# Attention scores in three banks, maxima moved by transfer alone, rows turned 13 images later

## The reference

```python
qkv = (xt @ W_fc.T + b_fc).reshape(bs, n, HEADS, 3 * D)
q, k, v = jnp.split(qkv, 3, axis=-1)
attn = jnp.einsum('bihd,bjhd->bijh', q, k) * scale
attn = jax.nn.softmax(attn, axis=2)
out = jnp.einsum('bijh,bjhd->bihd', attn, v).reshape(bs, n, HEADS * D)
out = out @ W_last.T + b_last + xt
```

## Time and profile before

| | us |
|---|---|
| three runs | 867.73, 867.62, 866.97 (median 867.62) |
| the profiled execution | 864.95 |
| its span, first to last instruction | 863.2 |
| PE busy, of the span | 688.5 (80%) |
| DVE busy | 612.1 (71%) |
| ACT busy | 418.2 (48%) |
| POOL busy | 424.5 (49%) |
| scores by query, first and last product start (L586) | 79.8 and 395.6 |

### The profile page before, as it was taken

One profiled execution on the slowest core, in us unless ns is written; L12 is line 12 of the kernel. 1 busy time (PEld: TensorE's weight loads), 2 busy tenths in 40 slices (PEclk: granted clock), 3 DMA queues, 4 the chain that ended last, 5 costly groups with the idle time before them and its releaser, 6 DMA issues. The chain is left out here.

```text
span 863.2 us, 21250 instructions
## 1 busy us (share of the span) xinstructions
PE 688.5 (80%) x7173; PEld 521.9 (60%) x7173; DVE 612.1 (71%) x1648; ACT 418.2 (48%) x829; POOL 424.5 (49%) x560
## 2 busy tenths in 40 slices
PE   0658899999999999997746998784988787359994
PEld 0234566666666666665545887762666666349993
DVE  3765578788877777876598888767567776647764
ACT  0355466665655544553264666520766666134442
POOL 0236102222227888879405777702555787724551
PEclk9979999999999999999566999985999999669995
DMA  6740000000000000000001222413400000122216
GB/s 175 225 164 1 2 3 2 3 3 3 2 3 4 3 15 15 21 16 21 25 1 34 53 53 54 47 7 106 119 2 2 14 17 17 53 68 72 65 46 195
DMA packets 42316, 37.39 MB, mean 43 GB/s; under 512 B 8947, under 2 KB 34536, under 8 KB 42212
## 3 DMA queue, kind: packets, MB, share of 16 engines
q1 hardware_dynamic: 35300, 24.55, 10.0%
q0 software_dynamic: 4800, 9.40, 4.8%
q10 hardware_dynamic: 2112, 2.10, 0.8%
HBM read 26.76 MB, written 9.46 MB: 42 GB/s over the span
## 5 line engine op out<-in xcount | busy, mean ns | idle before, releaser
L782 DVE TENSOR_REDUCE attend_negmax<-ps 128x4 f32<-128x1024 f32 (+1 forms) x128 | 139.6, 1090 | 82.9 <-PE ps L586 82.2
L729 ACT ACTIVATE attend_prob<-ps 128x1024 f32<-128x1024 f32 (+1 forms) x128 | 110.7, 865 | 137.2 <-PE ps L596 137.2
L586 PE MATMUL ps<-attend_key,attend_query 32*128 32x256 f32 (+2 forms) x1024 | 124.8, 360 | 12.8 <-DVE attend_negmax L782 11.6
L596 PE MATMUL ps<-attend_query,attend_key 32*128 32x256 f32 (+2 forms) x1024 | 124.6, 359 | 1.1 <-ACT attend_prob L729 1.0
L586 PEld LDWEIGHTS ps<-attend_key,attend_query 32*128 32x128 f32 x1024 | 79.6, 184 | 53.5 <-issue 45.7
L1777 POOL DMA_INDIRECT sums_xs<-table,sums_source x79 | 76.6, 969 | 56.8 <-DVE sums_source L1710 33.0
L596 PEld LDWEIGHTS ps<-attend_query,attend_key 32*128 32x128 f32 x1024 | 88.3, 184 | 2.3 <-issue 2.2
L1495 PE MATMUL ps<-sums_xT,sums_own 128*128 128x128 f32 x632 | 84.0, 279 | 0.0
L1495 PEld LDWEIGHTS ps<-sums_xT,sums_own 128*128 128x128 f32 x632 | 78.3, 195 | 0.0
L522 POOL TENSOR_SCALAR attend_rstd<-attend_spread 128x2 f32<-128x2 f32 x32 | 7.5, 234 | 130.7 <-DVE attend_spread L837 130.7
L1838 ACT ACTIVATE sums_hidden<-ps 128x512 f32<-128x512 f32 x79 | 47.2, 597 | 34.2 <-PE ps L1495 34.1
(11 more groups left out here) (346 smaller groups left out, 1616.7 us busy)
## 6 DMA issues: line engine op xcount, KB each, us to landing
attend_query<-attend_negmaxT SPq DMA_DIRECT2D x512, 0.5 KB
w<-in_L_ffn_w SPq DMA_DIRECT2D x1, 4096.0 KB, 27.9
expert_xs<-slots SPq DMA_DIRECT2D x39, 64.5 KB, 1.9
x<-in_x ACTq DMA_DIRECT2D x4, 512.0 KB, 8.3
table<-rows SPq DMA_DIRECT2D x16, 128.0 KB
experts<-in_L_ffn_W SPq DMA_DIRECT2D x1, 2048.0 KB, 8.7
experts<-in_L_ffn_W SPq DMA_DIRECT2D x4, 512.0 KB, 9.6
rows<-outputs SPq DMA_DIRECT2D x8, 256.0 KB, 4.9
```

The costliest lines, as they stand in the source:

```text
L586: return nc.tensor.matmul(ps[:, SCORE + i, at:at + width], query[rows, n % 3, odd, a * 128:(a + 1) * 128], key[rows, n % 3, odd, from_:fro ...
L596: return nc.tensor.matmul(ps[:, KEY_SCORE + i, at:at + width], key[rows, n % 3, odd, b * 128:(b + 1) * 128], query[rows, n % 3, odd, from_ ...
L729: nc.scalar.activation(of_pair(t // 4, t % 4)[:, :, 0:wide], ps[:, KEY_SCORE:KEY_SCORE + 2, 0:wide], ACT.Exp).then_inc(prob_ready, 1)
L782: last = nc.vector.tensor_reduce(out=negmax[:, s % 2, 0:4].rearrange("p (a r) -> p r a", a=2), in_=ps[:, SCORE:SCORE + 2, 0:2 * width].rea ...
```

## The change

Both kinds of scores get three banks in turn where banks are free: scores by query use banks 0 to 2 throughout; scores by key use 3, 4 and 7 in the first 48 slots, and 3 and 4 after that. TensorE then waits for one head of the slot before instead of for both, VectorE reduces each head by itself, and ScalarE takes the exponentials head by head in the first 48 slots. Bank 7 is TURN: the dense layer's rows are turned 13 images later instead of 5, and the gate's logits use it too. VectorE no longer transposes the maxima: SyncE sends them straight from 128 partitions into the query's row, in the dense layer two transfers a slot of 128 pieces of two numbers (query columns are then read in steps of two), in the windowed layer four of 128 pieces of one number. ScalarE copies the values out at j = 0, and their bias is multiplied by the output weights once, in the preparation, and added to the output's bias. The gate's products move from j = 2 to j = 0 and their copy from j = 3 to j = 1.

```diff
-    SCORE, KEY_SCORE, PROJECT, HEADS, TURN, MISC = 0, 2, 4, 5, 6, 7
+    SCORE, KEY_SCORE, PROJECT, HEADS, TURN = 0, 3, 5, 6, 7
+    KEY_BANKS = (KEY_SCORE, KEY_SCORE + 1, TURN)
+    BY_HEAD = 4 * (IMAGES - 4)
+    BEHIND = 13
...
+        def key_bank(t, i):
+
+            return KEY_BANKS[(2 * t + i) % 3] if t < BY_HEAD else KEY_SCORE + i
+
+        def exponentials(t):
+
+            return 2 * min(t, BY_HEAD) + max(t - BY_HEAD, 0)
+
+        def score_bank(s, i):
+
+            return SCORE + (2 * s + i) % 3
+
...
+        def placed(k):
+
+            return 32 * min(k, IMAGES) + 64 * max(k - IMAGES, 0)
...
-                    sp.wait_ge(max_turned, s + 1)
                     for i in range(2):
                         row = free_row(groups[i], odd)
+                        sp.wait_ge(max_ready, 2 * s + i + 1)
+                        if not windowed(n):
+                            sp.dma_start(query[row:row + 1, n % 3, odd, :], negmax[:, s % 4, i, :])\
+                                .then_inc(max_placed[s % 4], 16)
+                            continue
                         for a in range(2):
                             sp.dma_start(query[row:row + 1, n % 3, odd, a * 128:(a + 1) * 128],
-                                         negmaxT[2 * a + i::32, s % 4, :]).then_inc(max_placed[s % 4], 16)
+                                         negmax[:, s % 4, i, a:a + 1]).then_inc(max_placed[s % 4], 16)
...
                         if s >= 1 and not windowed(n):
-                            pe.wait_ge(max_ready, s)
+                            pe.wait_ge(max_ready, 2 * s - 1)
...
-                        return nc.tensor.matmul(ps[:, SCORE + i, at:at + width],
-                                                query[rows, n % 3, odd, a * 128:(a + 1) * 128],
+                        own = slice(a * 128, (a + 1) * 128) if windowed(n) else slice(a, N, 2)
+                        return nc.tensor.matmul(ps[:, score_bank(s, i), at:at + width],
+                                                query[rows, n % 3, odd, own],
...
-                            pe.wait_ge(prob_ready, t)
+                            pe.wait_ge(prob_ready, 2 * t - 1 if t < BY_HEAD else exponentials(t))
...
                     if s >= 1:
-                        pe.wait_ge(max_ready, s)
+                        pe.wait_ge(max_ready, 2 * s - 1)
...
+                def free_turn(n):
+
+                    if n == IMAGES - 3:
+                        pe.wait_ge(prob_ready, exponentials(BY_HEAD))
+                    if n - 6 >= IMAGES:
+                        pe.wait_ge(rowsT_ready, min(n - 5 - IMAGES, IMAGES))
+                        pe.wait_ge(logits_taken, min(n - 5 - IMAGES, IMAGES))
+
+                def turn_in(k):
+                    pe.wait_ge(rows_ready, k + 1)
+                    if k >= 1:
+                        pe.wait_ge(in_ready, k)
+                    for a in range(2):
+                        mm = nc.tensor.transpose(ps[:, TURN, a * 128:(a + 1) * 128], rows[:, 2 * k + a, 0:C], ident)
+                    mm.then_inc(in_turned, 1)
...
+                        if runs(n - 6) and windowed(n - 6):
+                            gate_logits(n - 6)
...
-                        if runs(n - 6) and windowed(n - 6):
-                            gate_logits(n - 6)
-                        if runs(n - 5):
+                        if n >= BEHIND:
+                            free_turn(n)
+                        if 0 <= n - BEHIND < IMAGES:
+                            turn_in(n - BEHIND)
+                        if runs(n - 5) and windowed(n - 5):
                             turn_rows(n - 5)
...
+                def take_values(n):
+                    act.wait_ge(v_projected, n + 1)
...
+                    for a in range(2):
+                        last = nc.scalar.activation(
+                            vaug[:, n % 3, a, :, :, 0:16],
+                            ps[:, PROJECT, a * 128:(a + 1) * 128].rearrange("p (r g d) -> p g r d", g=2, d=D), ACT.Copy)
+                    last.then_inc(vaug_ready, 1)
+
                 def exponential(t):
...
+                    if t < BY_HEAD:
+                        for i in range(2):
+                            act.wait_ge(key_scored[i], t + 1)
+                            nc.scalar.activation(to[:, i], ps[:, key_bank(t, i), 0:wide], ACT.Exp)\
+                                .then_inc(prob_ready, 1)
+                    else:
+                        for i in range(2):
+                            act.wait_ge(key_scored[i], t + 1)
+                        nc.scalar.activation(to, ps[:, KEY_SCORE:KEY_SCORE + 2, 0:wide], ACT.Exp).then_inc(prob_ready, 1)
...
+                    if j == 0 and runs(n):
+                        take_values(n)
                     if j == 3:
-                        if runs(n - 5):
+                        if 0 <= n - BEHIND < IMAGES:
+                            take_in(n - BEHIND)
+                        if runs(n - 5) and windowed(n - 5):
                             take_rows(n - 5)
...
-                    last = nc.vector.tensor_reduce(out=negmax[:, s % 2, 0:4].rearrange("p (a r) -> p r a", a=2),
-                                                   in_=ps[:, SCORE:SCORE + 2, 0:2 * width].rearrange(
-                                                       "p r (a n) -> p r a n", a=2),
-                                                   axis=AX.X, op=ALU.max, negate=True)
-                    last.then_inc(max_ready, 1)
-
-                def turn_max(s):
-                    dve.wait_ge(max_ready, s + 1)
-                    if s >= 4:
-                        dve.wait_ge(max_placed[s % 4], 64 * (s // 4))
-                    nc.vector.transpose(negmaxT[:, s % 4, :], negmax[:, s % 2, :]).then_inc(max_turned, 1)
+                    for i in range(2):
+                        dve.wait_ge(scored[i], s + 1)
+                        nc.vector.tensor_reduce(out=negmax[:, s % 4, i, :],
+                                                in_=ps[:, score_bank(s, i), 0:2 * width].rearrange(
+                                                    "p (a n) -> p a n", a=2),
+                                                axis=AX.X, op=ALU.max, negate=True).then_inc(max_ready, 1)
...
                 def add_out(n):
                     dve.wait_ge(out_projected, n + 1)
+                    dve.wait_ge(vaug_ready, min(n + 5, COUNT))
...
+                    pe.wait_ge(biased, 2)
+                    nc.tensor.matmul(ps[:, 5, 0:C], v_bias[:], wo[0][:], start=True, stop=True).then_inc(turned, 1)
...
                     dve.wait_ge(turned, 2)
+                    nc.vector.tensor_copy(v_bias[:], ps[:, 4, 2:3].to_broadcast([128, 128])).then_inc(biased, 1)
...
-                    nc.vector.tensor_copy(v_bias[:], ps[:, 5, 0:128])
+                    dve.wait_ge(turned, 3)
+                    nc.vector.tensor_tensor(o_bias[:, 0, :], o_bias[:, 0, :], ps[:, 5, 0:C], ALU.add)
```

More of the change, by code:

```diff
@@ L362, in _, with attend @@
                             widen(b)
-def attend(nc, xf, tokens, rows, table, weights, consts, query_scales, key_scales, v_bias, o_bias, window_mask, gate,
+def attend(nc, xf, tokens, rows, table, weights, consts, query_scales, key_scales, o_bias, window_mask, gate,
            logits, choice, ps):
@@ L415, in attend @@
         vaug_ready = sem("vaug_ready")
-        scored = sem("scored")
+        scored = [sem(f"scored{i}") for i in range(2)]
         max_ready = sem("max_ready")
-        max_turned = sem("max_turned")
         max_placed = [sem(f"max_placed{r}") for r in range(4)]
-        key_scored = sem("key_scored")
+        key_scored = [sem(f"key_scored{i}") for i in range(2)]
         prob_ready = sem("prob_ready")
@@ L758, in _ @@
             def _(dve):
-                def take_values(n):
-                    dve.wait_ge(v_projected, n + 1)
-                    if n >= 4:
-                        dve.wait_ge(out_projected, n - 3)
-                    if n == 0:
-                        dve.wait_ge(zeros_set, 3)
-                    if n >= 3:
-                        dve.wait_ge(weighted, 2 * n - 4)
-                    for a in range(2):
-                        out = vaug[:, n % 3, a, :, :, 0:16]
-                        got = ps[:, PROJECT, a * 128:(a + 1) * 128].rearrange("p (r g d) -> p g r d", g=2, d=D)
-                        if windowed(n):
-                            last = nc.vector.tensor_copy(out, got)
-                        else:
-                            last = nc.vector.tensor_tensor(
-                                out, got, v_bias[:].rearrange("p (r g d) -> p g r d", g=2, d=D), ALU.add)
-                    last.then_inc(vaug_ready, 1)
@@ L867, in _ @@
                     if j == 1:
-                        if runs(n):
-                            take_values(n)
                         if runs(n - 3):
                             invert_sums(n - 3)
+                        if runs(n - 6) and windowed(n - 6):
```

(21 more changed lines are left out.)

73 lines of the change are left out of this document (38 added, 35 removed).

## The result

The changed kernel takes 875.6 us (874.92 to 877.11, four runs) against 867.3 before: 1.0106 times as long, 95% interval 1.0079 to 1.0133. The forecast was 848.2, the range 835 to 868. It is slower, by the mechanism of the rival that named SyncE.

The account below looks back on a forecast made before the run. TensorE was taken to set the pace, its gaps being waits for the previous slot's maximum. Dense −11.4, windowed −12.0, lags +3 and preparation +1 sum to −19.4 us, taking the median from 867.62 to 848.2; range 835 to 868.

Parts of the forecast that it names:

- the rival that named SyncE: Windowed layer: at 0.61 us a transfer SyncE needs 10.9 us an image, +19 there, 878 us in all; chance 0.08.
- SyncE's price: Windowed layer: 0.43 us for each of 16 transfers, so SyncE needs 8.0 us an image, under 8.5.
- The dense layer: Dense layer: waits for the maximum, their drains and the turned rows go, ScalarE's lateness costs +0.3 an image; −11.4 us in all.
- the lags: VectorE meets its maxima at j = 0 and 2 behind other work: 0.1 us for each of 32 images, +3.
- each drain: TensorE drains and refills around each wait for the maximum, estimated at 0.1 us, to go with the wait.
- The windowed layer without SyncE's bound: Windowed layer: two waits of 0.38 and their drains go, −12.0 us in all, 8.5 us an image in the middle.
- The hold of 0.3 behind ScalarE's work at j = 3: Dense image: ScalarE's first half exponential ends some 0.3 us after TensorE could want the bank; charged +0.3 an image.
- The half reductions: VectorE, dense image: two reductions of 0.68 us replace one of 1.22, four times, +0.57 an image.
- Strided weights: Dense scores by query: loads of queries in steps of two numbers stay at 184 ns, bounds 184 and 368.
- The rival's price: Weights in steps cost 368 ns, four loads in 64 slots: 47 us, up to 895, half hidden 871; chance 0.05.
- The pieces in flight: Transfers of 128 pieces at 10 ns a packet: at most 2.6 us on one engine, 0.16 on 16; lower bound costs nothing.
- The preparation: Before the images: gains a copy, a product and an addition, loses a copy and a product; +1.0 us, bounds 0 and 1.5.

## Why the prediction was wrong, step by step

- **The step that failed** is SyncE's price: "a transfer costs between 0.43 and 0.61; I take 0.43, the row with the same number and size of pieces". It is 0.601, and the sum of 8.0 an image became 11.6. The row had the same number and size of pieces, but it was another kind of transfer: it reads the chip's main memory (an input of the kernel) and writes 128 partitions, while the maxima are read from 128 partitions. It was not cheap for want of a transfer ahead of it: it stood third in an unbroken row of issues, and loads that follow others further on cost 0.43 to 0.44 too. From SyncE's timeline of the kernel before:
```profile
1.27 0.42 SPq L2253 DMA_DIRECT2D const_prep<-in_const_prep  x1
...
9.00 0.44 SPq L2261 DMA_DIRECT2D wqk<-in_L_attn_Wk  x1
9.49 0.43 SPq L2262 DMA_DIRECT2D wv<-in_L_attn_Wv  x1
```
For the maxima it does matter what stands ahead. In the changed kernel an issue after a pause takes 0.47 (the least of the dense row above), one right behind another of its kind 0.60, and in a stage where 16 follow each other only the second counts. Why a load from main memory does not pay this, no run shows. SyncE already stood at 9.0 of 9.4 to 9.8 us in my own sum, so 0.1 us on each of 16 transfers could not be hidden. And the wait that was to cover it, "The maximum's wait for the transfers of four slots earlier has a slot's time in hand", is the one by which SyncE's backlog reached VectorE: 30.1 of 80 us in the view of waits above.
- **The rival** with this mechanism gave 10.9 us an image and 878 us; measured are 11.6 and 875.6. It missed the stretched issues (0.6 to 0.7 an image). That its +19 for the windowed layer came out is in part luck: images 17 to 19 still ran at 8.7 to 8.9, which makes up for those 0.7. So is its 0.61, which is the price of a load from main memory. It had a chance of 0.08; "128 pieces instead of four" deserved more.
- **The dense layer** came out near its sum: the waits for the maximum are gone, images take 9.17 where 9.3 was forecast. The forecast of −11.4, or −9.8 with its share of the lags, stands against −12.1. By parts it is −2.5 for images 0 to 2 (forecast −3), −2.1 for 3 and 4 (−1.0), −7.4 for 5 to 12 (−6.4) and −0.2 for 13 to 15 (−1.0), so misses partly cancel. Images 13 to 15 kept 10.07. The run with two banks for keys, where images 3 to 12 take as long without turning any rows, shows that they lack the third bank and the exponentials by head. It also shows that my sum had the gain in the wrong place: taking off the waits for the maximum brought nothing there, while the scores by key had two banks. No run shows the 0.1 us for each drain: the waits of 0.26 and 0.34 and the 0.31 of the turned rows alone make 0.91 of the 0.92 that an image lost.
- **The windowed layer without SyncE's bound** was close: 8.68, and 9.04 with the gate, against "8.5 in the middle". From image 16 to 31 the run with turned maxima gains 9.3 us, where −12.0 was forecast (two waits of 0.38 and two drains of 0.1 make 0.96 an image, not the 0.9 I took). In all it gives −23 (forecast for the whole change −19.4), because the lags of 3 do not show.
- **Lags**: the 0.1 an image that I charged does not show in the dense layer. The hold of 0.3 behind ScalarE's work at j = 3 does not show either: in the image shown, TensorE's line has no wait there, as the ends of its products are modelled.
- **The half reductions** take 687 and 553 ns (dense, windowed), ScalarE's halves 599 and its copies 274, all near their terms. From the groups by shape of 120 to 200 us:
```profile
L836 DVE TENSOR_REDUCE attend_negmax<-ps 128x2 f32<-128x512 f32 x71 | 45.8, 687 | 11.6 <-PE ps L609 10.5
...
L789 ACT ACTIVATE attend_prob<-ps 128x512 f32<-128x512 f32 x70 | 38.1, 599 | 23.5 <-PE ps L619 23.5
L619 PEld LDWEIGHTS ps<-attend_query,attend_key 32*128 32x128 f32 x280 | 25.2, 184 | 0.0
L609 PEld LDWEIGHTS ps<-attend_key,attend_query 32*128 32x128 f32 x280 | 24.8, 191 | 11.6 <-issue 7.3 <-DVE attend_negmax L836 2.7
...
L776 ACT ACTIVATE attend_vaug<-ps 128x128 f32<-128x128 f32 x18 | 4.0, 274 | 0.3
```
- **Strided weights** cost nothing that counts: 191 ns for queries in steps of two, 184 for keys without steps, and 189 for queries without steps in the windowed layer. By the rule of the Trainium skill ("SBUF — State Buffer", "Door 1: The DMA port swizzle") that two hits in a line give full rate, it would be so; the trace agrees to within these 7 ns. The rival's price was too low: the trace of the kernel before has 32 such loads a dense image, 8 a slot and not four, so 184 ns more for each would have made up to 94 us and not 47.
- **The pieces in flight** are no bound: they land 2.0 us after the issue. What they cost was the issuing.
- **The preparation** is +0.8 at image 0 in the changed kernel and +0.2 to +1.0 in the other runs that share it (forecast +1.0). The new product, L2342, comes after two waits:
```profile
22.37 1.44 PE L2338 MATMUL ps<-const_all,wide_bias 1*128 1x1 f32 x6 [3.00 <-DVE wide_bias L2374]
24.19 0.80 PE L2342 MATMUL ps<-wo,v_bias 128*128 128x128 f32 x2 [0.38 <-DVE v_bias L2377]
```

## What to carry to other kernels

Before a transfer is cut up or reshaped, add up what the issuing engine needs in one period of the loop, and see how much room is left. Take the price from a transfer of the same kind (between the same memories, from as many partitions) that stands behind another; the same number and size of pieces is not enough. If no row has that, the upper end of the range belongs in the forecast, or one run to measure it. When all engines get idler at once, read the issues, which the busy columns don't count.

## What had not been expected of the hardware

- The price of an issue on SyncE follows the partitions that a transfer reads: 0.492 for four partitions 16 or 32 apart, 0.573 for four that are 1 to 8 apart, 0.468 for two 64 apart, 0.559 for two neighbours, 0.626 for eight, 0.562 for 31, 0.567 for 62, and 0.59 to 0.60 for 16, 32, 64, 124 and 128. With 128 it is 0.47 after a pause; with four, 32 apart, a pause changes nothing (least and median are both 492 in the earlier trace rows). Why, no run shows.
- About one issue an image is stretched, in the changed kernel to 1.0 to 1.7 us. Each of the 16 such issues of maxima there between 232 and 400 us starts within 0.6 us of a load of program code (a packet of 16 KB on queue q8 that takes 0.9 to 1.6 us). There are 17 such loads, and the one without a stretched issue of maxima, at 394.2, meets the transfer of the rows, which is stretched too:
```profile
394.26 1.24 SPq L505 DMA_DIRECT2D table<-rows  x1
```
In the run with 124 pieces the loads come as often (seven from 260 to 330 us) and no windowed issue of maxima is longer than 0.86.
Two issues of the changed kernel from 297.2 us on, the second stretched to 1.407, and the code load between 297.4 and 299.7 us:
```profile
L500 SPq DMA_DIRECT2D attend_query<-attend_negmax x2: 599/1003/1407, 297.2 to 297.8; - x2
```
```profile
q8 instruction: 1, 0.02, 2.6%
```
In the two runs with other shapes only those of 16, 32, 64 and 128 partitions have issues over 1.0, those of 2, 4, 8, 31, 62 and 124 have none. By the Trainium skill ("DMA: Bandwidth & Descriptors", "Why a DMA increments its semaphore by 16 and not by 1") the first go to 16 engines and the others to 8 or fewer. That a code load holds up one of 16 engines and SyncE behind it fits all this, but was not tried by moving the loads.
- The granted clock of TensorE, 1.00 in the same stage of the kernel before, averages 0.96 from 275 to 395 us of the changed kernel, where TensorE waits: it is at the lower of its two levels (0.50, 1.2 GHz) from 343.8 to 347.1 and from 384.8 to 391.4 us. SyncE issues on through both stretches: between the starts of images 20 and 30 it stands idle for 0.3 of 115.6 us. So the clock can have added little to the 19 us; how much was not measured.
